# Feed-forward of a two-block transformer kernel: rounding, a quarter of the inner columns and the residual sum moved to POOL, the output copied out by ACT

## The reference, cut to what matters

```
def bitlinear(x, W, b):            # QB = 127, EPS = 1e-5
    w_scale = clip(mean(abs(W)), EPS)
    Wq = clip(round(W / w_scale), -1, 1) * w_scale
    x_scale = clip(max(abs(x), axis=-1), EPS)          # one number per row
    xq = clip(round(x * (QB / x_scale)), -QB - 1, QB) * (x_scale / QB)
    return xq @ Wq.T + b
ffn(x) = bitlinear(gelu(bitlinear(x, W1, b1)), W2, b2)  # W1: 1024 x 256, W2: 256 x 1024
x = x + ffn(layernorm(x))
x = x + latent_attention(ctx, layernorm(x), ...)        # its tokens are normalised rows of x
```

## Time and profile before

| | us |
|---|---|
| median of 3 runs | 927.55 |
| the profiled execution | 928.22 |
| its span in the profile | 926.5 |
| PE busy | 866.8 (94%) |
| DVE busy | 630.7 (68%) |
| ACT busy | 532.6 (57%) |
| POOL busy | 388.9 (42%) |

### The profile page before, as it was taken

How to read it: one execution, slowest core, us unless ns; L and a number is a source line. 1 busy time by engine, 2 the same in 40 slices (tenths; PEclk the granted TensorE clock), 3 DMA queues, 4 the chain that set the end, 5 groups by cost and what they waited for, 6 DMA issues and landing times.

```text
span 926.5 us, 14997 instructions
## 1 busy us (share of the span) xinstructions
PE 866.8 (94%) x4299; PEld 611.3 (66%) x4300; DVE 630.7 (68%) x1275; ACT 532.6 (57%) x851; POOL 388.9 (42%) x334
## 2 busy tenths in 40 slices
PE   9977789889999999999999999999999999999992
PEld 4635455545555555555457887878888888888881
DVE  5788987855567557456488779846666666666666
ACT  2558885445665765775554534326666666666650
POOL 2144455435676746756515545512222222222210
PEclk9999999989999999999999999999999999999997
DMA  9400000009478578569565100078711298526405
GB/s 310 110 1 1 0 1 1 1 5 364 160 292 328 194 305 326 219 269 350 199 262 196 82 1 1 12 316 342 305 40 36 71 348 341 208 88 254 116 9 182
DMA packets 49909, 154.07 MB, mean 166 GB/s; under 512 B 6266, under 2 KB 24438, under 8 KB 44236
## 3 DMA queue, kind: packets, MB, share of 16 engines
q1 hardware_dynamic: 46124, 144.25, 41.4%
q0 software_dynamic: 3744, 9.31, 3.1%
HBM read 97.85 MB, written 56.62 MB: 167 GB/s over the span
## 4 chain that ended last, share of the span: by engine, by line
PE 67%; DVE 17%; ACT 6%; issue 3%; DMA 3%; POOL 2%; SPq 1%; DVEq 0%; ACTq 0%; POOLq 0%
PE banks L1047 11%; PE banks L1300 8%; PE banks L1302 8%; PE banks L1301 8%; PE banks L1015 4%; PE banks L1039 3%; PE banks L1040 3%; DVE small L2105 2%; PE banks L1337 2%; PE banks L1339 2%; PE banks L1338 2%; PE banks L1313 2%; PE banks L953 2%; PE banks L919 1%; PE banks L1061 1%
## 5 line engine op out<-in xcount | busy, mean ns | idle before, releaser
L1047 PE MATMUL banks<-wexp 128*65 128x512 f32 (+1 forms) x288 | 149.9, 602 | 3.5 <-ACT wexp L1614 3.5
L677 POOL TENSOR_TENSOR cv_hl<-wexp,cv_hl 128x1024 fp32r<-128x1024 f32 x45 | 108.6, 2421 | 56.0 <-ACT cv_hl L1591 55.4
L1300 PE MATMUL banks<-ring,x_hi 128*128 x312 | 127.5, 408 | 0.0
L1302 PE MATMUL banks<-ring,x_lo 128*128 x312 | 122.1, 391 | 0.0
L1301 PE MATMUL banks<-ring,x_hi 128*128 x312 | 122.0, 391 | 0.0
L1614 ACT ACTIVATE wexp<-banks 128x512 f32<-128x512 f32 x128 | 76.4, 599 | 64.2 <-PE banks L1040 63.8
L2105 DVE TENSOR_REDUCE small<-banks 128x1 bf16<-128x1107 f32 x64 | 84.1, 1314 | 38.4 <-PE banks L1015 38.4
L1750 ACT ACTIVATE banks<-wexp 128x1024 f32 x72 | 73.5, 1021 | 47.7 <-DVE aux L2496 47.7
L1728 ACT ACTIVATE aux<-banks 128x512 f32<-128x512 f32 x78 | 46.7, 599 | 61.2 <-PE banks L1302 45.2
L1039 PE MATMUL banks<-q_hi,k_hl 128*128 128x512 f32 x144 | 76.7, 533 | 1.9 <-ACT q_lo L1582 1.0
L1302 PEld LDWEIGHTS banks<-ring,x_lo 128*128 128x128 f32 x312 | 58.6, 188 | 13.2
(11 more groups left out here) (374 smaller groups left out, 2171.5 us busy)
## 6 DMA issues: line engine op xcount, KB each, us to landing
wsplit<-cv_hl SPq DMA_DIRECT2D x45, 1024.0 KB, 8.0
ring<-wsplit SPq DMA_DIRECT2D x32, 1280.0 KB
wexp<-in_L_ffn_w SPq DMA_DIRECT2D x40, 512.0 KB, 5.9
wexp<-in_expert_biases SPq DMA_DIRECT2D x8, 1152.0 KB, 6.6
ring<-wsplit SPq DMA_DIRECT2D x4, 1024.0 KB, 8.2
wexp<-moe_y SPq DMA_DIRECT2D x7, 512.0 KB, 6.1
wexp<-in_L_ffn_sw SPq DMA_DIRECT2D x5, 512.0 KB, 9.0
x_sb<-in_x SPq DMA_DIRECT2D x4, 512.0 KB, 7.6
```

Of the source, the lines that this page charges most:

```text
L677: g.tensor_tensor(sides(hl[:, PIECE:2 * PIECE]), raw, sides(hl[:, 0:PIECE]).bitcast(f32), ALU.subtract).then_inc(s['cv_lo'], 1)
L1047: mm(pb[5 + half][0:DA, :], vh[b][0:w, c, :], pT[q % 3][0:w, :], start=c == 0, stop=c == len(KTILES) - 1).then_inc(s['a_pv'], 1)
L1300: mm(o[:], x_hi[u][:, kc, :], hi, start=kc == 0 and not primed, stop=False, skip_group_check=primed)
L1302: last = mm(o[:], x_lo[u][:, kc, :], hi, start=False, stop=primed and kc == KC - 1, skip_group_check=primed)
```

## The change

POOL takes three new instructions per tile, and ACT one new in place of one and a quarter:

- the rounding of the tokens moves from ACT to POOL (ACT keeps it for the last tile only);
- of the 1024 inner columns ACT rounds the first 768 and POOL the last 256, with a semaphore of its own (`f_hmP`) for which PE waits too;
- the output of tile t is copied out of PSUM by ACT, scaled, into `y_part`, and POOL adds it to x (`f_res`); DVE's `ffn_sum` is gone;
- a row tile's statistics stand one turn later in DVE's queue, behind the inner values instead of ahead of the largest values;
- POOL normalises as x * rstd + less_mean, where DVE makes less_mean = -mean * rstd (one instruction more for each half of the tiles);
- semaphores `warm`, `w_inv` and `ctx_n` are joined with others, which leaves each wait where it was.

```diff
+        HA = 3 * HID // 4
 # POOL
+            def ffn_tokens(t):
+                g.tensor_scalar(xn[:, t % 2, :], xn[:, t % 2, :], f_by[:, t % 2, 0:1], MAGIC, ALU.mult, ALU.add).then_inc(s['f_xm'], 1)
+            def ffn_hidden(t):
+                pool.wait_ge(s['f_by'], t + 4)
+                h = h_f[t % 2][:, HA:HID]
+                g.tensor_scalar(h, h, f_by[:, 1 - t % 2, 1:2], MAGIC, ALU.mult, ALU.add).then_inc(s['f_hmP'], 1)
+            def ffn_result(t):
+                pool.wait_ge(s['f_yout'], t + 1)
+                g.tensor_tensor(x_sb[:, t, :], x_sb[:, t, :], y_part[t % 2], ALU.add).then_inc(s['f_res'], 1)
             for t in range(T):
                 if t >= 2:
                     pool.wait_ge(s['f_xqT_full'], t - 1)
-                g.tensor_scalar(xn[:, t % 2, :], x_sb[:, t, :], mv[:, t, 0:1], rstd[:, t:t + 1], ALU.subtract, ALU.mult).then_inc(s['f_xn'], 1)
+                g.tensor_scalar(xn[:, t % 2, :], x_sb[:, t, :], rstd[:, t:t + 1], less_mean[:, t:t + 1], ALU.mult, ALU.add).then_inc(s['f_xn'], 1)
+                if t >= 1:
+                    pool.wait_ge(s['f_by'], t)
+                    ffn_tokens(t - 1)
+                if t >= 4:
+                    ffn_hidden(t - 4)
                 pool.wait_ge(s['f_xn'], t + 1)
-                if t >= 5:
-                    pool.wait_ge(s['f_by'], t)
                 g.tensor_tensor(x_sb[:, t, :], x_sb[:, t, :], b2_all[:], ALU.add).then_inc(s['f_pool'], 1)
+                if t >= 6:
+                    ffn_result(t - 6)
+            ffn_hidden(T - 4)
             ...  (the 15 short steps)
             pool.sem_inc(s['f_pool'], 1)
+            for t in range(T - 6, T):
+                if t + 3 < T:
+                    ffn_hidden(t + 3)
+                ffn_result(t)
             for u in range(2):
                 ...  (the memsets)
 # PE, ffn_hidden_T
+                pe.wait_ge(s['f_hmP'], t + 1)
 # ACT
-                if there(tokens):
+                if isinstance(tokens, int) and tokens == T - 1:
                     a(xn[:, u, :], xn[:, u, :], ACT.Copy, scale=f_by[:, u, 0:1], bias=MAGIC).then_inc(s['f_xm'], 1)
-                    a(h_f[1 - u], h_f[1 - u], ACT.Copy, scale=f_by[:, u, 1:2], bias=MAGIC).then_inc(s['f_hm'], 1)
+                    a(h_f[1 - u][:, 0:HA], h_f[1 - u][:, 0:HA], ACT.Copy, scale=f_by[:, u, 1:2], bias=MAGIC).then_inc(s['f_hm'], 1)
+            def ffn_sum(t, u):
+                act.wait_ge(s['f_y'], t + 1)
+                act.wait_ge(s['f_by'], t + 5)
+                if not isinstance(t, int) or t >= 2:
+                    act.wait_ge(s['f_res'], t - 1)
+                a(y_part[u], pb[6][:, 0:D], ACT.Copy, scale=f_step[:, 1 - u, 1:2]).then_inc(s['f_yout'], 1)
             def ffn_turn(i, u):
                 if there(i + 3):
                     ffn_T(i + 3, 1 - u)
+                if there(i - 1):
+                    ffn_sum(i - 1, 1 - u)
 # DVE
-            def ffn_sum(t, u): ...
             def ffn_turn(i, u):
-                if there(i - 1):
-                    ffn_sum(i - 1, 1 - u)
                 if there(i + 1):
                     ve.wait_ge(s['f_acc'], i + 2)
                 if there(i + 3) or there(i):
+                    if not isinstance(i, int) or i >= 2:
+                        ve.wait_ge(s['f_yout'], i - 1)
                     last = v.tensor_tensor(f_step[:, 1 - u, c], f_max[1 - u][:, c], wsc[:, c], ALU.mult)
-                if there(i - 1):
-                    ffn_statistics(i - 1)
                 ...
                 if there(i + 2):
                     ffn_hidden(i + 2, u)
+                if there(i - 2):
+                    last = ffn_statistics(i - 2)      # waits for f_res
+            link(ffn_statistics(T - 1))               # after the last turn
```

More of the change, by code:

```diff
@@ L192, in program @@
         h_qT = [scr.take(HID, HC, bf16) for _ in range(2)]
+        y_part = [scr.take(D) for _ in range(2)]
         assert scr.at <= mark
@@ L272, in program @@
         ln_r = sb("ln_r", [P, T])
+        less_mean = sb("less_mean", [P, T])
         gateT = sb("gateT", [P, KC, E])
@@ L327, in program @@
         eno, eno_sh = sb("eno", [P, 1]), sb("eno_sh", [P, 1])
[L329 removed]
+        names = """ld_x ld_l0 ld_ffn ld_l1 ld_route ld_w0 ld_w1 ld_w2 ld_bias1 w_ready cv_hi cv_lo const ld_x1 ld_x2 ld_x3 ld_w12 w_times prep_full prep_free prep_dve w_abs
             root_in root_out chain chain_pool
             g_xn g_xnT_full g_xnT g_sc g_sh g_p g_pT_full g_pT g_av
[L332 removed]
+            f_rstd f_xn f_by f_hm f_hmP f_xm f_xqT_full f_xqT f_acc f_pre f_h f_amax f_hqT_full f_hqT f_y f_yout f_res f_pool a_const a_q
             l_free l_xh l_xT_full l_xT l_qkv l_qk l_sq l_ss l_bo
@@ L582, in _ @@
             g.memset(ones[:], 1.0)
-            g.memset(ones_b[:], 1.0).then_inc(s['warm'], 1)
+            g.memset(ones_b[:], 1.0).then_inc(s['const'], 1)
             link(g.memset(ident[:], 0.0))
@@ L789, in warm @@
                     mm(pb[7][:], ones_b[:], ones_b[:].unsqueeze(1).to_broadcast([P, 4, P]), start=True, stop=True)
-            pe.wait_ge(s['warm'], 1)
+            pe.wait_ge(s['const'], 2)
             warm(28)
-            pe.wait_ge(s['const'], 2)
+            pe.wait_ge(s['const'], 3)
             pe.wait_ge(s['ld_l0'], NLD['ld_l0'])
@@ L820, in turn_ctx @@
             def turn_ctx():
-                pe.wait_ge(s['ctx_n'], 1)
+                pe.wait_ge(s['prep_dve'], 1)
                 o = bank()
@@ L1449, in kept @@
                 last.then_inc(s['prep_free'], 1)
-            act.wait_ge(s['const'], 2)
+            act.wait_ge(s['const'], 3)
             ready(ACT.Sqrt)
@@ L1470, in times @@
             def times(k, raw):
-                act.wait_ge(s['w_inv'], 1)
+                act.wait_ge(s['prep_dve'], 2)
                 a(flat(raw), flat(raw), ACT.Copy, scale=winv[:, k:k + 1], bias=MAGIC).then_inc(s['w_times'], 1)
@@ L1809, in norm @@
                 link(v.reciprocal(d, t_))
-            ve.wait_ge(s['const'], 2)
+            ve.wait_ge(s['const'], 3)
             link(v.tensor_scalar(eno_i[:], eno_i[:], 31, None, ALU.bitwise_and))
@@ L1887, in context_tokens @@
                                            ALU.subtract, ALU.mult)
-                last.then_inc(s['ctx_n'], 1)
+                last.then_inc(s['prep_dve'], 1)
             def ternary():
@@ L1893, in ternary @@
                 link(v.tensor_scalar(wsc, wabs, 1.0 / (HID * D), QEPS, ALU.mult, ALU.max))
-                v.reciprocal(winv, wsc).then_inc(s['w_inv'], 1)
+                v.reciprocal(winv, wsc).then_inc(s['prep_dve'], 1)
             def masks():
@@ L1911, in ffn_scales @@
                 norm(t0, t1, 0.0)
-                ve.sem_inc(s['f_rstd'], 1)
+                v.scalar_tensor_tensor(less_mean[:, t0:t1], mv[:, t0:t1, 0], -1.0, rstd[:, t0:t1], ALU.mult, ALU.mult).then_inc(s['f_rstd'], 1)
             def attended(it):
@@ L1983, in ffn_hidden @@
                 v.scalar_tensor_tensor(h_f[u], banks[:, 2 * (1 - u) * 512:2 * (2 - u) * 512], f_step[:, u, 0:1], b1_all[:], ALU.mult, ALU.add).then_inc(s['f_acc'], 1)
[L1985 to L1989, removed]
             def ffn_statistics(t):
-                ve.wait_ge(s['f_yout'], t + 1)
-                statistics(t)
+                ve.wait_ge(s['f_res'], t + 1)
+                return statistics(t)
             def ffn_turn(i, u):
-                if there(i - 1):
-                    ffn_sum(i - 1, 1 - u)
                 if there(i + 1):
@@ L2002, in ffn_turn @@
                     c = slice(0 if there(i + 3) else 1, 2 if there(i) else 1)
+                    if not isinstance(i, int) or i >= 2:
+                        ve.wait_ge(s['f_yout'], i - 1)
                     last = v.tensor_tensor(f_step[:, 1 - u, c], f_max[1 - u][:, c], wsc[:, c], ALU.mult)
-                    if not there(i + 1):
+                    if isinstance(i, int) and i < 0:
                         link(last)
-                if there(i - 1):
-                    ffn_statistics(i - 1)
+                    elif not there(i + 1):
+                        last.then_inc(s['f_by'], 1)
+                        ve.wait_ge(s['f_by'], i + 5)
                 if there(i + 4):
@@ L2017, in ffn_turn @@
                     ffn_hidden(i + 2, u)
+                if there(i - 2):
+                    last = ffn_statistics(i - 2)
+                    if isinstance(i, int) and i == T - 7:
+                        link(last)
             ss_l = p0[:].rearrange("p a b -> p (a b)")
@@ L2041, in between @@
                     ffn_scales(TB, T)
-                if i == T - 8:
+                if i == T - 7:
                     aggregate(0, LN_EARLY)
```

## The result

The changed kernel takes **931.14 us** (median of 5 runs, 930.58 to 932.67), the kernel before on the same chip 927.55 (5 runs, 926.71 to 930.71): ratio **1.0032, 95% interval 1.0019 to 1.0046**, so some 3.0 us slower (1.8 to 4.3); the two medians differ by 3.6. Forecast were 7.9 us more, within 927 to 943. The direction and the main cost hold; the size was more than twice what was measured.

The account below looks back on a forecast made before the run. The prediction took rings between DVE, ACT, PE and POOL to bound the turns. Turns -1.7, short steps +0.8, hand-over +7.8 and low clock +1.0 gave +7.9, so 935.4 us, range 929.4 to 941 (8 in 10: 927 to 943).

Parts of the forecast that it names:

- DVE-ACT: Ring in a steady turn: DVE's inner values, ACT's gelu, DVE's largest value to the next reciprocal; 3.92 us.
- PE-ACT: Ring in a steady turn: PE's transposes, ACT's copies including the new output copy, PE's multiplication by W2; 3.94 us.
- The hand-over: To the next layer: POOL's memsets and first tiles behind the last result delay the ninth tile's tokens; 7.8 us lost.
- The tail: Last turns: POOL's 15 short steps run later and delay the next layer's first tokens; 0.8 us lost (0 to 1.2).
- the size of the turns: Eleven steady turns: 4.06 us each, 46.2 instead of 47.9 in all; a gain of 1.7 us.
- b = 0.50: Time in us of each POOL rounding in a turn; at 0.50 nothing is lost (3.92), at the assumed 0.60 4.06.
- the first turns: Start of the turns: ACT's 0.42 gained once, two less_mean instructions of about 0.2 each paid on DVE; net 0.
- the clock term: Behind PE's waits at the next layer's start: a spell mostly at 1.2 GHz costs 1.0 us (0 to 2.4).
- slow POOL: Rival: POOL's multiply-add takes 1.22 like its subtract form and bounds the turns at 5.1; 947 us; chance 0.12.
- The swallowed hand-over: Rival: PE doesn't run dry at the next layer's start, only the turns' gain counts; about 925 us; chance 0.14.
- Blocked turns: Rival: POOL's full queue holds DVE's L2003 and L1976 every turn, turns stay at 4.35; 938.5 us; chance 0.05.
- cancelling: Rival: turns of 3.92 (gain 5) and the hand-over at its low end offset each other; 928 us; chance 0.07.

Follow-up runs that it names:

- e4: The changed kernel (plus e0's clamp) with POOL's normalisation back as subtract and multiply; 932.88 us, ratio 1.0037 to the kernel before.
- e3: The kernel before, with only POOL's memsets moved behind the wait for the last output; 934.88 us, ratio 1.0074 to the kernel before.
- e9: e2 with tile 10's result add ahead of the 15 short steps and memsets split behind the adds of tiles 11 and 12; 923.8 us, ratio 0.9954 to before.
- e5: The changed kernel (plus e0's clamp) with the tokens rounded on ACT again; 934.51 us, ratio 1.0047 to the kernel before.
- e7: The changed kernel (plus e0's clamp) with tokens and all inner columns rounded on ACT again; 936.27 us, ratio 1.0074 to the kernel before.
- e1: The changed kernel (plus e0's clamp) with POOL's memsets moved behind the result add of tile 10; 929.12 us, ratio 1.0008 to the kernel before.
- e2: e1 with the next layer's first two tiles and the third's bias add between POOL's last result adds; 924.3 us, ratio 0.996 to the kernel before.
- e0: The changed kernel with two registers clamped at zero before PE and ACT wait on them in the last stage; 930.95 us, ratio 1.0027 to before.
- e11: The same kernel as e2, run on another chip; 924.35 us, ratio 0.9952 to the kernel before.

## Why the prediction was right in kind and wrong in size

**Right.** The bound was read as rings between engines, and in the changed kernel's trace DVE-ACT decides, with the gelu waiting for the inner values and PE-ACT within 0.1 of it. POOL's multiply-add was taken at 0.60 between ends of 0.40 and 1.22; it is 0.48 (L615, L620) and 0.55 (L631), and e4 shows the slow end belongs to the other form. The hand-over was named as the main cost and sized at 7.8: 7.13, and e3 has 6.2 without the rest. Of the 0.7 too much, 0.44 is the way from the fourth square to the ninth tile's tokens, 6.16 instead of 6.6. The tail was 0.2 too dear.

**Wrong, and by how much.** The step that failed first is the size of the turns. The prediction let POOL's bias add hold the step multiply and with it the turn, 4.06 instead of 3.92, which left a gain of 1.7 for all turns. With the roundings at 0.48 instead of 0.60 the bias add starts and ends 0.28 earlier, at 1.16 to 1.88 behind the reciprocal instead of 1.43 to 2.16, and the gelu wait covers what is left: 0 instead of 0.14 a turn. The prediction said that b = 0.50 loses nothing, and took 0.60. The ten turns from tile 2 to 12 lost 2.60 (40.65 against 43.25), 0.26 each, which is the difference of the two rings, 4.19 - 3.92.

The first two turns differ from these by a low-clock spell. Each trace has one there, behind PE's long wait. Before, it began with the transposes, 1.61; now these took 1.06, and the spell (granted clock 0.52 from 71.0 to 74.4, against 0.56 in the earlier trace rows) fell on the multiplications behind them. So it lengthened both turns before (4.85 and 4.68 for 4.19) and only the second now (3.93 and 5.08 for 3.92): 1.15 and 1.17 in all. Twelve turns of 0.26 are 3.1, where the prediction had 1.7. That the first of them alone shows 0.92 is luck of where the spell fell: in e9, built alike up to there, it began with the transposes, and the first turn took 4.74 (the last line, of e9; above it the changed kernel's PE).

```profile
69.30 1.06 PE L945 MATMUL banks<-ident,wexp 128*128 128x128 f32 x8 [2.39 <-POOL wexp L620]
71.06 1.89 PE L935 MATMUL banks<-wexp,aux 128*128 128x512 bf16 x4 [0.47 <-ACT aux L1531]
68.99 1.94 PE L967 MATMUL banks<-ident,wexp 128*128 128x128 f32 x8 [2.40 <-POOL wexp L620]
```

The second is the start, in the sentence on the first turns: "gain ACT's 0.42 once and pay for two less_mean instructions", 0. The first rounding starts 0.48 earlier (68.17 against 68.65). The 0.42 is there: it starts 0.20 behind the reciprocal instead of 0.62, and 0.61 behind it in e5 and e7, where ACT rounds the tokens again. The price isn't: the reciprocal is 0.06 earlier (67.97 against 68.03). DVE did have idle time, 0.51 before, and the second less_mean stands in it (before, then changed):

```profile
66.18 0.16 DVE L2003 TENSOR_TENSOR small<-small 128x1 f32<-128x1 f32 x1 [0.51 <-DVE small L1809]
65.71 0.36 DVE L1947 SCALAR_TENSOR_TENSOR less_mean<-small 128x8 f32<-128x8 f32 x1
```

The third is the clock term, 1.0 for the spell behind PE's wait: 0. The spell came (4.06 instead of 2.75 at 150.11), but a wait of 0.81 for the ninth tile stands behind it and takes it up; the tokens there come from DVE, which waits for POOL's squares and not for PE. "Only the last one lies on the path" was wrong: behind the last wait, of 0.81, no spell came. e1 shows the term where its condition holds, a wait of 2.53 right ahead of the path: 1.3 us.

Together 1.4 for the turns, 0.5 for the start and 1.0 for the clock, with the 0.7 and 0.2 above, are the 3.8.

The rivals: slow POOL is refuted by L615 and e4. The swallowed hand-over is refuted by PE's 5.38; its 925 is near what e2 measures (924.3) once the queue's order is changed. Blocked turns are refuted by the turns. Of the times put on record cancelling (928) is the nearest to 931.14, but not by its terms: the hand-over did not come in at its low end of 5.0.

What stays open: how large the gain of the turns is over many executions, since each trace is one. From the rounding of tile 0 to that of tile 12 the two traces with the old turns have 52.78 (before) and 54.03 (e3), the six with the changed ones (changed kernel, e0, e1, e2, e9, e11) 48.87 to 51.10, with e2 and e9 at the ends for where the first spell fell.

## What to carry to other kernels

When work moves to an engine with slack, its queue order is what you pay for: list what used to run in that slack (here 3.75 us of memsets and two tiles of the next stage), and place it before a wait for the last result, not behind; in e2 that was worth 6.2 to 6.7 us, where the shorter turns and the earlier start were worth 3.6 in the traces. Write down every ring between the engines, not only the longest; a part that is worth little alone can be what lets another pay. In these traces a low-clock spell behind a wait cost time where the path ran on through PE (e1, 1.3 us), and none where PE had to wait for another engine once more behind it (the changed kernel).

## What the runs showed of the hardware

- POOL's TENSOR_SCALAR on 128x256 takes 1.21 to 1.22 with subtract and multiply by two columns, 0.55 with multiply and add of two columns, 0.48 with multiply by a column and add of a constant.
- A memset on POOL holds DVE's TENSOR_SCALAR: four of them took 2.63 beside memsets, 1.37 without (e1 against the changed kernel), though a memset reads no tensor. POOL's two-input instructions do so too: in the changed kernel one at 148.38 took 1.19 beside a square of 1.04, where one alone takes 0.41. The Trainium skill (SBUF — State Buffer, section Who interferes with whom) says that tensor_scalar on VectorE can take the port pair that it shares with GpSimd, and that whichever issues first keeps it for its whole instruction; the trace agrees, 2.63 against 1.37, with the fourth of e1 as long as the memset that began 0.15 before it, 1.18.
- Equal idle times of PE were not followed by equal spells: after 2.39 eight transposes took 1.06 (changed kernel), after 2.40 they took 1.94 (e9).
- After idle times of 4.4 and 5.4 us PE's next eight multiplications of 512 columns took 4.97 and 4.06 instead of 2.75, at granted clocks of 0.50 (e3) and 0.66 (changed kernel); after 0.81 and 1.25 they took 2.75.
